# An attention and expert-layer block: operands turned by transposing transfers, and scatters that wait for their landings alone

## The chip, the cores and the metric

The kernel runs on one core of a Trainium2 chip. The metric is the device time of one execution in microseconds (us).

## What is computed

The input x has 8 batches of 512 tokens, each of 128 numbers. The block is attention without weight matrices, a layer norm, a routed expert layer with a shared expert beside it, and a second layer norm.

```python
xh = x.reshape(8, 512, 16, 8)                      # 16 heads of 8
c  = xh - mean(xh, axis=1)
p  = softmax(einsum('bthd,bThd->bhtT', c, c))
x  = layernorm(x + einsum('bhtT,bThd->bthd', p, xh))   # "x1" in the kernel

scores = sigmoid(x @ gate_weight.T)                # 64 experts
# top 4 of 8 groups by (scores + bias), then the top 8 experts of them
# a token gets a slot of an expert while fewer than 128 tokens have one, in the order of tokens
ye  = (silu(xe @ w1.T) * (xe @ w3.T)) @ w2.T       # for each expert, its 128 slots
out = sum over a token's 8 experts of weight * ye
out = out + (silu(x @ sg.T) * (x @ su.T)) @ sd.T   # shared expert
x   = layernorm(x + out)
```

## The kernel before

Every instruction is placed by hand on its engine, and engines wait for each other's counters (semaphores). A counter of a transfer rises by 16 when the transfer has landed. Each engine, SP's queue of transfers included, does its list strictly in order.

**Stage 1, attention and routing, batch after batch.** TensorE, ScalarE and VectorE run through batches b = 0 to 7. In a batch, TensorE makes 32 blocks of scores (`score`, L664), two matmuls of 512 columns each, into four banks S, so that two blocks are in flight. ScalarE takes each with one exponential (L913) into `large`, and TensorE weighs the values with it (`weigh`, L678) into PV. A batch has 16 slots of two scores; at fixed slots (`SLOT_OF`) TensorE does small jobs into two other banks, M[0] and M[1] (`BANK`): for the next batch q = b + 1 the mean (`mean`), the largest norm (`most`) and the turned operands (`lr0` to `lr7`), and for the previous batch p = b - 1 what leads to its routing (`xt`, `logits`, `gate`, `up`, `down`, `pos`, `totals`). A job waits until the reader of the job before it in its bank is through.

The operands of the scores are split in three bf16 parts. VectorE writes them for batch q into AK and AQ (`prep_parts`, `prep_rows`; the last step is `l40`), tokens on partitions. The scores need them with tokens along the row: job `lr`j turns two heads of both by 8 transposing matmuls (L582) into a bank, and VectorE (six of them, `take_turned`, L1173) or ScalarE (j = 3 and 6, L891) copies the bank into LR. The copies of j = 0 to 7 happen while LR's earlier columns are still read by the scores of batch b.

For batch p, VectorE computes x1 (L1187), the scores of the experts, the top 8, and at its end the slot numbers `index` (L1314). Then GpSimd writes the batch's records with 32 indirect transfers of 128 rows each (`scatter`, L506): a record is x1, the 64 weights and the token's number. GpSimd copies x1 into the record (L495) and makes the number (L496, L498). Each transfer waits for two things:

```python
wait(pool, exp_done, min(CHUNKS * (p + 2) + i * TOP + k - 4, CHUNKS * BATCHES))
landed = scattered[p % 2][k % 2]
wait(pool, landed, scatters_before(p) + 16 * ((i * TOP + k) // 2))
```

that is, until ScalarE has done a certain exponential of batch p + 2, and until the transfer two before it has landed. There are two record buffers; VectorE writes x1 of batch p once GpSimd has copied x1 of batch p - 1. A record whose slot number is out of bounds is dropped by the transfer; the experts' 128 slots fill up in the early batches.

**SP** loads x, clears `records` and `sums` in device memory, loads w1, w3 and w2 (L407 to L409), and then stores Z of each batch p (x1 plus the shared expert, L414) when VectorE has written it.

**Stage 2.** TensorE turns the experts' weights (L783), with ScalarE and VectorE copying them, while GpSimd still scatters. **Stage 3** begins when all scatters have landed: SP loads the slots of four experts at a time (L424), 16 steps; GpSimd adds the results to `sums` (L526). **Stage 4** is the last sum and layer norm.

## Time and profile before

| | |
|---|---|
| median of 3 runs | 682.28 us (682.13 to 687.41) |
| the profiled execution | 683.21 us, of which 681.5 us are the span of the trace |
| TensorE busy | 418.1 us, 61% of the span |
| GpSimd busy | 384.5 us, 56% |
| ScalarE busy | 382.2 us, 56% |
| VectorE busy | 343.8 us, 50% |
| chain that ended last | TensorE 23%, GpSimd 22%, ScalarE 20%, issue 17%, VectorE 15% |

The busy shares are means over stages that have different limits, so the view by stages says more than the table. In the trace PE is TensorE, PEld its weight loads, ACT ScalarE, DVE VectorE, POOL GpSimd, and SPq the queue of SP. "Issue" in the chain is time in which an engine waited for nothing that the profile shows.

### The profile page before, as it was taken

What the parts mean: (1) busy time and instruction counts of PE and PEld (TensorE: products, weight loads), DVE (VectorE), ACT (ScalarE), POOL (GpSimd) and SP (SyncE); (2) the same over time, 40 slices, a digit from 0 to 9 for tenths busy, and PEclk for the clock granted to TensorE, in tenths of its full rate; (3) what the DMA queues carried; (4) which work ended last, traced back from release to release, by engine and by line L of the source; (5) the groups of instructions that cost most, each with busy time, mean ns of one, the idle gap of its engine ahead of it and who ended that gap; (6) DMA issues with size and microseconds to landing.
All of it is one profiled execution on the core that took longest, in us unless ns stands there. A gap on an engine that the chain in (4) does not pass through costs nothing.

```text
span 681.5 us, 9076 instructions
## 1 busy us (share of the span) xinstructions
PE 418.1 (61%) x2948; PEld 194.5 (29%) x2948; DVE 343.8 (50%) x1118; ACT 382.2 (56%) x516; POOL 384.5 (56%) x424
## 2 busy tenths in 40 slices
PE   4788978968978878788798833352005546653000
PEld 4223323323322323232232212242005545542000
DVE  5514765766757757757742831863003343333065
ACT  2898958968969969879779931023003322210026
POOL 2000005566666667557566567566660888888846
PEclk9999979989979989989989975577557767675555
DMA  3899971110000000000000000000006555444498
GB/s 93 203 241 295 178 149 49 36 27 8 10 22 7 6 20 4 5 19 3 4 20 3 19 2 2 18 1 1 1 1 183 104 83 87 52 36 37 41 265 227
DMA packets 83125, 43.66 MB, mean 64 GB/s; under 512 B 13319, under 2 KB 82707, under 8 KB 83072
## 3 DMA queue, kind: packets, MB, share of 16 engines
q1 hardware_dynamic: 61568, 36.18, 22.2%
q0 software_dynamic: 21504, 6.81, 8.8%
q8 instruction: 29, 0.48, 0.3%
q14 instruction: 24, 0.20, 0.1%
HBM read 21.27 MB, written 44.40 MB: 96 GB/s over the span
## 4 chain that ended last, share of the span: by engine, by line
PE 23%; POOL 22%; ACT 20%; issue 17%; DVE 15%; DMA 3%; SPq 0%; ACTq 0%; POOLq 0%; DVEq 0%
ACT large L913 14%; POOL sums L526 14%; POOL records L506 8%; PE PV L678 8%; PE S L664 5%; PE M L582 2%; ACT OT L898 2%; PE M L570 1%; PE PV L688 1%; PE M L611 1%; DVE LR L1173 1%; PE M L605 1%; PE S L582 1%; DVE last_stats L1502 1%; DVE left L1267 1%
## 5 line engine op out<-in xcount | busy, mean ns | idle before, releaser
L506 POOL DMA_INDIRECT records<-rec,index x256 | 254.4, 994 | 175.7 <-ACT large L913 78.9
L913 ACT ACTIVATE large<-S,shift_now 128x1024 f32<-128x1024 f32 x256 | 274.7, 1125 | 59.6 <-PE S L664 59.1
L678 PE MATMUL PV<-large,V 128*9 128x512 f32 x1024 | 139.5, 618 | 0.2 <-ACT large L913 0.2
L526 POOL DMA_INDIRECT sums<-centred,target x64 | 99.9, 1561 | 35.8 <-issue 18.9
L664 PE MATMUL S<-LR 64*128 64x512 bf16 x512 | 101.5, 398 | 21.9 <-ACT large L913 19.0
L664 PEld LDWEIGHTS S<-LR 64*128 64x128 bf16 x512 | 24.4, 93 | 164.8 <-ACT large L913 123.0
L982 ACT COPY AK<-S 128x512 f32<-128x512 f32 x16 | 9.3, 583 | 67.2 <-PE S L792 67.2
L1173 DVE COPY LR<-M 128x1024 bf16<-128x1024 bf16 x42 | 28.7, 684 | 34.9 <-PE M L582 34.9
L792 PE MATMUL S<-ident,X 128*128 128x128 f32 x64 | 14.4, 369 | 48.5 <-DMA X<-records 48.5
L495 POOL COPY rec<-x 128x512 f32<-128x512 f32 x7 | 4.9, 699 | 67.0 <-DVE x L1187 67.0
L810 PE MATMUL PV<-ident,AK 128*128 128x128 f32 x32 | 9.0, 375 | 44.3 <-DVE AK L1444 44.3
L1469 DVE CAST target<-number 128x4 uint32<-128x4 f32 x16 | 2.7, 171 | 63.7 <-DMA sums<-centred,target 62.8
L688 PE MATMUL PV<-ident,OT 128*128 128x128 f32 x128 | 21.0, 286 | 14.1 <-ACT OT L898 14.1
L1021 ACT ACTIVATE last_log<-last_moments,eps 128x4 f32<-128x4 f32 x8 | 2.4, 297 | 46.5 <-DVE last_moments L1505 46.5
L997 ACT ACTIVATE X<-X 128x256 f32<-128x256 f32 x16 | 6.7, 417 | 36.7 <-DVE X L1433 36.7
L1458 DVE COPY weight<-X 128x4 f32<-128x4 f32 x16 | 2.6, 160 | 48.0 <-DMA X<-records 48.0
L816 PE MATMUL M<-large,AK 128*128 128x256 f32 (+1 forms) x64 | 26.4, 560 | 0.0
L792 PEld LDWEIGHTS S<-ident,X 128*128 128x128 f32 x64 | 11.4, 195 | 51.9 <-issue 50.3
L678 PEld LDWEIGHTS PV<-large,V 128*9 128x9 f32 x1024 | 15.2, 88 | 32.4 <-issue 28.5
L1071 DVE RECIPROCAL rden<-PV 128x16 f32<-128x16 f32 x32 | 8.1, 253 | 32.4 <-PE PV L688 32.4
L801 PE MATMUL S<-large,AK 128*128 128x128 f32 (+1 forms) x128 | 23.4, 343 | 0.0
L582 PE MATMUL M<-ident_b,AK 128*128 128x128 bf16 x224 | 22.9, 227 | 0.0
(184 smaller groups left out, 737.6 us busy)
## 6 DMA issues: line engine op xcount, KB each, us to landing
records<-blank SPq DMA_DIRECT2D x1, 6176.0 KB, 30.1
X<-records SPq DMA_DIRECT2D x16, 386.0 KB, 3.5
large<-sums SPq DMA_DIRECT2D x24, 256.0 KB, 4.7
sums<-blank SPq DMA_DIRECT2D x2, 2112.0 KB
large<-L_ffn_w_dram SPq DMA_DIRECT2D x2, 2048.0 KB, 21.3
records<-rec,index POOLq DMA_INDIRECT x256
X<-L_attn_x_dram SPq DMA_DIRECT2D x8, 256.0 KB, 2.8
sums<-Z SPq DMA_DIRECT2D x8, 256.0 KB
```

What stands on the lines that cost most here:

```text
L506: pool.indirect_dma_start(records, bass.IndirectOffsetOnAxis(ap=index[:, i * TOP + k:i * TOP + k + 1], axis=0), rec[:, i, :], None, bounds ...
L526: pool.indirect_dma_start(sums[n % SUMS], bass.IndirectOffsetOnAxis(ap=target[:, u, i:i + 1], axis=0), ye[:, u, i, :], None, bounds_check= ...
L582: mm = pe.transpose(bank[:, side * TOKENS + i * P:side * TOKENS + (i + 1) * P], A[:, i, 2 * j:2 * j + 2, :].rearrange("p a c -> p (a c)"), ...
L664: mm = pe.matmul(S[:, 2 * (n % 2) + j, :], LR[rows, pair, 0, tile * P:(tile + 1) * P], LR[rows, pair, 1, :], start=True, stop=True)
L678: mm = pe.matmul(PV[g % 2][32 * i:32 * i + VCOLS, :], V[:, 2 * c + k, QUAD * g + i, :], E[:, u % 2, i, k, :], start=c == 0 and k == 0, sto ...
L688: mm = pe.transpose(PV[g % 2][:, i * P:(i + 1) * P], OT[:, i * P:(i + 1) * P], ident[:, :])
L792: mm = pe.transpose(S[:, u % 2, i * CAP:(i + 1) * CAP], slots_in[:, u % 4, i * REC:i * REC + DIM], ident[:, :])
L801: mm = pe.matmul(S[:, 2 + u % 2, i * P:(i + 1) * P], xeT[:, u % 2, i * CAP:(i + 1) * CAP], w13_flat[:, bass.ds((GROUP_OF * s + i) * P, P)] ...
L816: mm = pe.matmul(M[u % 2][:, 2 * r * DIM:(2 * r + 2) * DIM], ehT[:, u % 2, r * CAP:(r + 1) * CAP], w2bd_flat[:, bass.ds((2 * s + r) * 2 * ...
L898: nc.scalar.copy(OT[:, :], PV[g % 2][:, :]).then_inc(quad_copied, 1)
L913: nc.scalar.activation(E[:, u % 2, 2 * (i // 2):2 * (i // 2) + 2, i % 2, :], S[:, 2 * (n % 2):2 * (n % 2) + 2, :], ACT.Exp, bias=shift_now ...
L1173: v.tensor_copy(LR[:, j, :, :].rearrange("p a t -> p (a t)"), Mb[bank]).then_inc(read[bank], 1)
```

## The change

Turning the operands moves from TensorE to SP. For each batch q from 1 on, SP issues two transposing transfers (`dma_start_transpose`, one for AK and one for AQ, each 128 partitions by 4096 bf16), once VectorE's `l40` of q is done and once the last score of batch q - 2 is done, since there are now two buffers LRs. Batch 0 is turned by TensorE as before. Jobs `lr0` to `lr7` go, with their copies on VectorE and ScalarE. TensorE waits at the start of a batch for both transfers (`turned`), and so does VectorE before it overwrites AK and AQ. `most` moves from slot 10 and bank 0 to slot 12 and bank 1. Z has two buffers and its store a counter for each. VectorE writes x1 and the number straight into the record, once the scatters of batch p - 2 have landed. GpSimd's copies go, and a scatter waits for `index` and for the landing of the one two before it; the wait for an exponential is gone.

```diff
-BANK = {"mean": 1, "lr0": 0, "lr1": 1, "xt": 0, "gate": 1, "logits": 0, "up": 0, "lr2": 1, "down": 0, "most": 0, "lr3": 1,
-        "pos": 0, "lr4": 1, "totals": 0, "lr5": 1, "lr6": 0, "lr7": 1}
-SLOT_OF = {"mean": 0, "lr0": 3, "lr1": 4, "xt": 5, "logits": 6, "gate": 6, "up": 7, "lr2": 9, "down": 9, "most": 10, "lr3": 11,
-           "pos": 12, "lr4": 13, "totals": 13, "lr5": 14, "lr6": 15, "lr7": 15}
+BANK = {"mean": 1, "xt": 0, "gate": 1, "logits": 0, "up": 0, "down": 0, "most": 1, "pos": 0, "totals": 0}
+SLOT_OF = {"mean": 0, "xt": 5, "logits": 6, "gate": 6, "up": 7, "down": 9, "most": 12, "pos": 12, "totals": 13}
-ACT_TAKES = {3: 11, 6: 15}
...
-PREP_JOBS = [name for name in SLOT_OF if name in ("mean", "most") or name.startswith("lr")]
+PREP_JOBS = ["mean", "most"]
...
-        AK = sb("AK", [P, TILES, HEADS, HEAD_ROWS], BF16)
-        AQ = sb("AQ", [P, TILES, HEADS, HEAD_ROWS], BF16)
-        LR = sb("LR", [P, HEADS // 2, 2, TOKENS], BF16)
+        A = sb("A", [P, 2, TILES, HEADS, HEAD_ROWS], BF16)
+        AK, AQ = A[:, 0, :, :, :], A[:, 1, :, :, :]
+        LRs = [sb(f"LR{k}", [P, 2, TILES, HEADS // 2, P], BF16) for k in range(2)]
...
@@ -408,11 +400,23 @@
+            def turn(q):
+
+                sp.wait_ge(prep, prep_at(q, "l40"))
+                if q >= 2:
+                    sp.wait_ge(scored, CHUNKS * (q - 1))
+                for side in range(2):
+                    sp.dma_start_transpose(LRs[q % 2][:, side, :, :, :].rearrange("p i j t -> p (i j) t"),
+                                           A[:, side, :, :, :].rearrange("p i h c -> p (i h c)")).then_inc(turned, 16)
+
+            turn(1)
             for q in range(BATCHES):
+                if q + 2 < BATCHES:
+                    turn(q + 2)
                 bank, n = job("epilogue" if q == BATCHES - 1 else "last" if q == BATCHES - 2 else "mid", q + 1, "down")
                 sp.wait_ge(read[bank], n + 1)
                 sp.dma_start(sums[0][q * TOKENS:(q + 1) * TOKENS, :].rearrange("(i p) d -> p i d", p=P),
-                             tokens_of(Z, q).rearrange("p (i d) -> p i d", i=TILES)).then_inc(dram_blank, 16)
+                             Z[:, q % 2, :, :]).then_inc(z_stored[q % 2], 16)
             for k in range(2):
...
@@ -488,19 +492,9 @@
             def scatter(p):
 
                 rec, index = record_of(p)
-                wait(pool, post, post_at(p, "x1_3"))
-                for t in range(2):
-                    wait(pool, scattered[p % 2][t], scatters_before(p))
-                if not last_of_all(p):
-                    nc.gpsimd.tensor_copy(rec[:, :, 0:DIM], x1[:, :, :]).then_inc(record, 1)
-                nc.gpsimd.tensor_copy(rec[:, :, TOK_COL], token[:, :]).then_inc(record, 1)
-                wait(pool, record, 3 * p + 3)
-                nc.gpsimd.tensor_scalar(token[:, :], token[:, :], float(TOKENS), None, ALU.add).then_inc(record, 1)
-                wait(pool, record, 3 * p + 4)
                 wait(pool, post, post_at(p, "index"))
                 for i in range(TILES):
                     for k in range(TOP):
-                        wait(pool, exp_done, min(CHUNKS * (p + 2) + i * TOP + k - 4, CHUNKS * BATCHES))
                         landed = scattered[p % 2][k % 2]
...
@@ -512,11 +506,11 @@
-            pool.wait_ge(small_ready, 3)
-            pool.sem_inc(record, 1)
             iterations(pool, batch)
             scatter(BATCHES - 1)
-            pool.wait_ge(dram_blank, 16 * (SUMS + BATCHES))
+            pool.wait_ge(dram_blank, 16 * SUMS)
+            for k in range(2):
+                pool.wait_ge(z_stored[k], 16 * BATCHES // 2)
 
...
@@ -583,17 +577,11 @@
-            def turn(phase, b, q, j):
-                if j == 0:
-                    wait_next(pe, prep, prep_at(q, "l40"))
-                m = begin(phase, b, f"lr{j}")
-                turn_into(Mb[m], j).then_inc(written[m], 1)
-
...
                     rows = slice(HEAD_ROWS * j, HEAD_ROWS * (j + 1))
-                    mm = pe.matmul(S[:, 2 * (n % 2) + j, :], LR[rows, pair, 0, tile * P:(tile + 1) * P],
-                                   LR[rows, pair, 1, :], start=True, stop=True)
+                    mm = pe.matmul(S[:, 2 * (n % 2) + j, :], LRs[b % 2][rows, 0, tile, pair, :],
+                                   LRs[b % 2][rows, 1, :, pair, :], start=True, stop=True)
                 mm.then_inc(scored, 1)
...
                 wait(pe, prep, prep_at(b, "shift"))
+                wait(pe, turned, 16 * 2 * b)
                 row_maxima(phase, b)
...
                                [:, :, lo:hi, :]).then_inc(v_built, 1)
-                bank, n = job(phase, b, f"lr{j}")
-                wait(act, written[bank], n + 1)
-                nc.scalar.copy(LR[:, j, :, :].rearrange("p a t -> p (a t)"), Mb[bank]).then_inc(read[bank], 1)
 
             def copy_quad(b, g):
...
             iterations(act, batch)
             copy_quad(BATCHES - 1, QUADS - 1)
             norm_start(BATCHES - 1)
             copy_x1T("epilogue", BATCHES)
-            act.wait_ge(post, post_at(BATCHES - 1, "x1_3"))
-            for t in range(2):
-                act.wait_ge(scattered[(BATCHES - 1) % 2][t], scatters_before(BATCHES - 1))
-            nc.scalar.copy(record_of(BATCHES - 1)[0][:, :, 0:DIM], x1[:, :, :]).then_inc(record, 1)
             exp_gate("epilogue", BATCHES, BATCHES - 1)
             exp_logits("epilogue", BATCHES, BATCHES - 1)
...
                 wait(dve, read[bank], n + 1)
+                wait(dve, turned, 16 * 2 * (q - 1))
                 x3 = xc[:, :].rearrange("p (g d) -> p g d", d=HD)
...
@@ -1182,9 +1151,12 @@
-                wait(dve, record, 3 * p + 1)
-                for i in range(TILES):
-                    t.step(f"x1_{i}", v.tensor_scalar(x1[:, i, :], O[:, i, :], moments[:, i, 0:1], rstd[:, i:i + 1],
+                rec, _ = record_of(p)
+                for way in range(2):
+                    wait_next(dve, scattered[p % 2][way], scatters_before(p))
+                t.step("number", v.tensor_scalar(rec[:, :, TOK_COL], rec[:, :, TOK_COL], 2.0 * TOKENS, None, ALU.add))
+                for i in range(TILES):
+                    t.step(f"x1_{i}", v.tensor_scalar(rec[:, i, 0:DIM], O[:, i, :], moments[:, i, 0:1], rstd[:, i:i + 1],
...
@@ -1273,8 +1245,10 @@
             def post_shared_out(phase, b, p):
                 bank, n = job(phase, b, "down")
                 wait_next(dve, written[bank], n + 1)
-                v.tensor_tensor(tokens_of(Z, p), M[bank][:, :], x1[:, :, :].rearrange("p i d -> p (i d)"), ALU.add
-                                ).then_inc(read[bank], 1)
+                wait(dve, z_stored[p % 2], 16 * (p // 2))
+                v.tensor_tensor(Z[:, p % 2, :, :],
+                                M[bank][:, :].rearrange("p (i d) -> p i d", i=TILES), record_of(p)[0][:, :, 0:DIM],
+                                ALU.add).then_inc(read[bank], 1)
...
                 rec, _ = record_of(p)
-                for way in range(2):
-                    wait_next(dve, scattered[p % 2][way], scatters_before(p))
...
-                    take_turned(phase, b, 2)
                 if with_post:
                     post_top(p, t)
                     post_shared_out(phase, b, p)
                     post_record(p, t)
+                leave(b, 1)
                 if with_prep:
                     take_most(phase, b, q)
-                leave(b, 1)
                 if with_post:
                     post_pos(phase, b, p, t)
-                if with_prep:
-                    take_turned(phase, b, 4)
                 if with_post:
                     post_totals(phase, b, p)
                 if with_prep:
-                    take_turned(phase, b, 5)
                     prep_shift(phase, b, q, w.step, w.after)
```

**SP's queue.** Around the end of the weight loads it held the following before (`w2n` is the last load of weights, Z the stored sum):

```order
12 L408 DMA large<-L_ffn_w_dram 64x64x128
13 L409 DMA w2n<-L_ffn_w_dram 128x64x64
14 L414 DMA sums<-Z 128x4x128 [waits read0] x8
15 L424 DMA X<-records 128x4x193 [waits scattered1_0,scattered1_1,scattered0_1,scattered0_0]
```

and now:

```order
12 L400 DMA large<-L_ffn_w_dram 64x64x128
13 L401 DMA w2n<-L_ffn_w_dram 128x64x64
14 L409 DMA_TRANSPOSE LR<-A 128x32x128 [waits prep]
15 L409 DMA_TRANSPOSE LR<-A 128x32x128
16 L409 DMA_TRANSPOSE LR<-A 128x32x128 [waits scored,prep]
17 L409 DMA_TRANSPOSE LR<-A 128x32x128
18 L418 DMA sums<-Z 128x4x128 [waits read0]
19 L409 DMA_TRANSPOSE LR<-A 128x32x128 [waits scored,prep]
```

The first pair, for batch 1, stands behind the clearing of the buffers and all loads of weights; the later pairs stand each ahead of a store of Z.

**TensorE's queue** in the later half of a middle batch (slots 9 to 11) before:

```order
134 L582 MATMUL M<-ident_b,AQ 128x128 x4
135 L624 MATMUL M<-small_T,hT 128x128 x4
136 L664 MATMUL S<-LR 128x512 x2
137 L678 MATMUL PV<-large,V 9x512 x4
138 L664 MATMUL S<-LR 128x512 x2
139 L688 MATMUL PV<-ident,OT 128x128 x4
140 L576 MATMUL M<-largest_diag,ones 128x128
141 L664 MATMUL S<-LR 128x512 x2
```

and now (slots 9 to 12):

```order
92 L612 MATMUL M<-small_T,hT 128x128 x4
93 L650 MATMUL S<-LR 128x512 x2
94 L664 MATMUL PV<-large,V 9x512 x4
95 L650 MATMUL S<-LR 128x512 x2
96 L674 MATMUL PV<-ident,OT 128x128 x4
97 L650 MATMUL S<-LR 128x512 x2
98 L664 MATMUL PV<-large,V 9x512 x4
99 L650 MATMUL S<-LR 128x512 x4
100 L664 MATMUL PV<-large,V 9x512 x4
101 L650 MATMUL S<-LR 128x512 x2
102 L570 MATMUL M<-largest_diag,ones 128x128
103 L622 MATMUL M<-mask_b,before_b 128x64 x2
```

The turning matmuls are gone, and the matmul of `most` no longer follows `down` at once in the same bank; it stands four scores later, ahead of `pos`.

**GpSimd's queue** at the first batch's scatters before (`rec` is the record, `index` the slot numbers):

```order
28 L495 COPY rec<-x 128x4x128 [waits records_blank,small_ready,post]
29 L496 COPY rec<-token 128x4
30 L498 TENSOR_SCALAR token<-token 128x4 [waits record]
31 L506 DMA records<-rec,index 8192x193 [waits exp_done,post,record]
32 L506 DMA records<-rec,index 8192x193 [waits exp_done]
33 L506 DMA records<-rec,index 8192x193 [waits scattered0_0,exp_done]
```

and now:

```order
28 L500 DMA records<-rec,index 8192x193 [waits post,records_blank]
29 L500 DMA records<-rec,index 8192x193
30 L500 DMA records<-rec,index 8192x193 [waits scattered0_0]
31 L500 DMA records<-rec,index 8192x193 [waits scattered0_1]
32 L500 DMA records<-rec,index 8192x193 [waits scattered0_0]
```

What is left on the queue is the transfers, each with one wait.

## Rows read from the trace of the kernel before

**Rows 1.** The page's busy tenths in 40 slices of the span.

```profile
PE   4788978968978878788798833352005546653000
POOL 2000005566666667557566567566660888888846
```

**Rows 2.** Busy time of each engine by stretch: batch 5, batch 7, two later stretches.

```profile
257.50:307.10 49.60, 41.58 (x321) 15.30 (x321) 33.03 (x105) 40.31 (x49) 31.60 (x33) 0.93 0.05 10
357.30:397.60 40.30, 34.48 (x252) 9.95 (x244) 21.68 (x81) 38.93 (x47) 24.91 (x28) 1.00 0.05 10
475.00:513.10 38.10, 0.00 (x0) 0.00 (x0) 0.00 (x0) 0.00 (x0) 25.25 (x26) 0.50 0.02 1
513.10:681.50 168.40, 64.92 (x288) 54.22 (x288) 64.85 (x256) 44.93 (x112) 116.87 (x120) 0.63 0.59 113
```

**Rows 3.** Timeline of VectorE and GpSimd around the scatters and the slot numbers.

```profile
102.22 0.18 DVE L1314 TENSOR_SCALAR index<-best 128x32 uint32<-128x32 f32 x1
...
103.72 1.23 POOL L506 DMA_INDIRECT records<-rec,index  x1 [29.46 <-ACT large L913]
...
393.64 0.22 DVE L1314 TENSOR_SCALAR index<-best 128x32 uint32<-128x32 f32 x1
...
416.52 1.12 DVE L1187 TENSOR_SCALAR x<-O,moments,rstd 128x128 f32<-128x128 f32 x4 [12.46 <-POOL token L498]
...
440.20 0.18 DVE L1314 TENSOR_SCALAR index<-best 128x32 uint32<-128x32 f32 x1
...
466.57 1.06 POOL L506 DMA_INDIRECT records<-rec,index  x1 [0.57 <-POOL token L498]
```

**Rows 4.** The chain that ended last, in order of time: start, us, what.

```profile
435.73 2.69 DMA records<-rec,index
...
467.63 0.30 issue
467.94 0.90 POOL records L506
468.84 0.73 issue
...
511.01 2.10 DMA records<-rec,index
```

**Rows 5.** Groups of instructions in batch 5 (257.5 to 307.1 us).

```profile
L913 ACT ACTIVATE large<-S,shift_now 128x1024 f32<-128x1024 f32 x32 | 34.4, 1124 | 9.1 <-PE S L664 9.0
...
L582 PE MATMUL M<-ident_b,AK 128*128 128x128 bf16 x32 | 3.4, 231 | 0.0
...
L576 PE MATMUL M<-largest_diag,ones 128*128 128x128 f32 x2 | 0.8, 488 | 4.2 <-DVE Z L1276 4.2
```

**Rows 6.** The exponentials' group in batch 7 (357.3 to 397.6 us).

```profile
L913 ACT ACTIVATE large<-S,shift_now 128x1024 f32<-128x1024 f32 x32 | 34.4, 1120 | 1.1 <-PE S L664 1.0
```

**Rows 7.** Timeline of ScalarE at the starts of batches 1, 5 and 7.

```profile
59.06 0.20 ACT L904 COPY shift_now<-shift 128x1 f32<-128x1 f32 x1
...
257.44 0.20 ACT L904 COPY shift_now<-shift 128x1 f32<-128x1 f32 x1
...
357.32 0.20 ACT L904 COPY shift_now<-shift 128x1 f32<-128x1 f32 x1
```

**Rows 8.** Timeline of SP's queue: the issue of the last weights.

```profile
70.74 11.22 SPq L409 DMA_DIRECT2D w2n<-L_ffn_w_dram  x1
```

**Rows 9.** Transfers from 90 to 106 us, in 40 slices of 0.4 us: busy tenths, GB/s.

```profile
DMA  9999999999999964795100000000000000000034
GB/s 202 230 220 223 218 246 207 218 228 225 223 220 212 189 123 87 228 285 169 26 20 12 0 0 0 0 0 0 0 0 0 0 0 0 0 0 0 0 116 131
```

**Rows 10.** Transfers of SP's queue, 66 to 82 us: packets, MB, share of 16 engines.

```profile
q1 hardware_dynamic: 5529, 2.82, 119.0%
```

**Rows 11.** Transfers of GpSimd's queue, 400 to 512 us.

```profile
q0 software_dynamic: 3600, 0.14, 2.1%
```

**Rows 12.** Timeline of VectorE: the last step of `prep_rows` in batch 5.

```profile
263.88 0.28 DVE L1158 COPY AK<-AQ 128x512 bf16<-128x512 bf16 x1
```

More of the change, by code:

```diff
@@ L244, in post_norm_block @@
         dram_blank = sem("dram_blank")
+        z_stored = [sem(f"z_stored{k}") for k in range(2)]
         written = [sem(f"written{o}") for o in range(2)]
@@ L254, in post_norm_block @@
         first_turned = sem("first_turned")
+        turned = sem("turned")
         first_taken = [sem(f"first_taken{o}") for o in range(2)]
@@ L929, in batch @@
                         build_v(b, HEADS - QUAD, HEADS)
-                    if phase != "last":
-                        for j, at in ACT_TAKES.items():
-                            if slot == at:
-                                take_turned(phase, b, j)
                     if phase != "first":
@@ L1392, in _ @@
             v.tensor_copy(slot_base[:, :], slot_base_i[:, :]).then_inc(small_ready, 1)
[L1393 removed]
+            for k in range(2):
+                v.tensor_scalar(recs[k][:, :, TOK_COL], token_i[:, :], float((k - 2) * TOKENS), None, ALU.add
+                                ).then_inc(small_ready, 1)
             v.tensor_copy(blank[:, TOK_COL:REC], blank_i[:, :]).then_inc(small_ready, 1)
```

47 lines of the change are left out of this document (15 added, 32 removed).

## The prediction

> **What bounds the kernel now.** I read the 40 slices first, then the stretches, then the chain. In the slices [rows 1] (17 us each, counted from 0) TensorE is busy through slice 22, thin after it, idle in 28 and 29, and busy again from 30, while GpSimd never stops from slice 6 to 29. So there are three bounds in turn. Up to 397.6 us the batches bound; from there to 513.1 us the scatters do (in the last 38.1 us of it no other engine did anything [rows 2]); after that comes an expert stage that the change does not touch, 168.4 us [rows 2].
>
> The scatters. The chain shows what one costs: a landing 2.10 us after the start, then 0.73 us until the waiting transfer starts [rows 4]. Each waits for the one two before it, so a pair takes 2.83 us and more; the last group's 31 steps from 466.57 to 511.01 us [rows 3, 4] are 1.43 us each, 2.87 us a pair, whatever GpSimd's own 0.97 us. The last batch's 32 scatters ran from 466.6 to 513.1 us: 46.5 us [rows 3, 4]. The first started at 103.7 us, 1.3 us after the first `index` was done at 102.4 us [rows 3]. From there to 513.1 us are 409.4 us; eight groups at 46.5 us are 372 us. The difference is the wait for exponentials, which ties a group to a batch of attention: batches 1 to 6 take (357.3 - 59.1) / 6 = 49.7 us each [rows 7].
>
> The batches. In batch 5 ScalarE waits 9.0 us for scores, in batch 7 1.0 us [rows 5, 6]. Batch 7 is the batch without `lr`, `mean` and `most` jobs, and it takes 40.3 us [rows 2]. So it is a row for what a batch costs when nothing is turned.
>
> **What the change removes.** Per middle batch: 64 turning matmuls (6.7 us of TensorE; the group shown is half of them, the other half took as long [rows 5]), eight copies, and the wait of 4.2 us of `most` for Z in bank 0 [rows 5], which goes with its move to bank 1. `mean` and `most` stay: 1.1 + 0.8 us of matmuls beside batch 7's 40.3 us. A batch then takes 42.2 us, 7.5 us less than 49.7 us. The copies on ScalarE and VectorE lie beside this and are in batch 7's figure. `index` of the previous batch is ready 393.9 - 357.3 = 36.5 us after batch 7's start [rows 3, 7], so 38.4 us after a middle batch's start. GpSimd's copies, about 1 us a group, go from the path; VectorE's one small step more is under 0.2 us and has the batch to hide in.
>
> **What it adds: a hole before batch 1.** TensorE now waits at the start of batch 1 for the first pair of transposing transfers. They stand on SP's queue behind the clearing and the weights, whose last issue ends at 70.7 + 11.2 = 82.0 us [rows 8]. The transfers already queued keep the DMA engines at nine tenths until 96.0 us [rows 9]. Batch 1 starts at 59.1 us now [rows 7]. So nothing of attention runs between the end of batch 0 and 96 us plus the pair's own time T. Everyone waits for that: TensorE, ScalarE behind its scores, VectorE at its overwriting of AQ, and with them `index` of batch 0, thus GpSimd. The Trainium skill, "DMA: Bandwidth & Descriptors", section "Queues, rings and completion order", says that each DMA engine consumes the descriptors of SP's ring in ring order; by that the pair cannot overtake the weights.
>
> **The price of a pair.** Both transfers move 2 x 128 x 4096 x 2 bytes = 2.10 MB. No row shows a transposing transfer. From below: the fastest slice moves 285 GB/s [rows 9], which gives 7.4 us. From above: if the pair went in pieces as small as the scatters' packets, 3600 of them carry 0.14 MB (39 bytes each) and take 2.1% of 16 engines in 112 us, 10.5 ns each [rows 11]; 53,800 of them make 35 us. Between them: the weight loads moved 2.82 MB in 16 us, 176 GB/s [rows 10], in packets of some 512 bytes; AK's rows of 128 values are 256 bytes, so this row is nearest. It gives 11.9 us; with one landing of 2.1 us I take T = 14 us.
>
> **What the pairs cost later.** Those of batches 2 to 7 are issued 6.7 us into the batch before (VectorE's last step of `prep_rows` ends at 264.2 us in a batch that began at 257.4 us [rows 7, 12]) and have the other 35.5 us to land: hidden up to T = 35.5 us. But from batch 3 on they run beside scatters. A scatter beside a store of Z landed after 2.69 us, not 2.10 us [rows 4], so a pair of scatters takes 3.46 us, not 2.87 us, and 14 us of transposing cost 14 x 0.59 / 3.46 = 2.4 us. Five of them: 12 us. From below this is nothing (the store may not have been what held that landing); at T = 35 us it is 30 us.
>
> **The sum.** Batch 1 starts at 96 + 14 = 110 us; `index` of batch 0 at 148.4 us; first scatter 1.3 us later, 149.7 us, where it was 103.7 us. The batches then gain: six at 42.2 us and one at 40.3 us end at 404 us, about where they ended before (397.6 us). But `index` of batch p comes every 42.2 us and its scatters take 46.5 us, so GpSimd never catches up and works through eight groups without a gap: 372 us, and 3 us for groups whose records still carry data (first batches) = 375 us. The queue of scatters also holds VectorE back: x1 of batch p needs the record buffer of p - 2, which from batch 5 on is free some us late, and this too is beside GpSimd's work. The last `index` is out well before group 7's turn at about 480 us. End of the scatters: 149.7 + 375 + 12 = 536.7 us, 23.6 us later than 513.1 us. The rest, 168.4 us, is as it was. The profiled execution took 683.2 us; with 23.6 us it is 706.8 us. It stands 0.9 us above the median, so the median becomes **706 us**. With T at its lower end, and nothing lost to the pairs, the sum is 7 + 12 = 19 us less, 687 us. At T = 35 us it is 21 + 18 = 39 us more, 745 us.
>
> **Rivals.** (a) *Transposing is so slow that it sets the period.* Beyond T = 35.5 us a batch is 6.7 us + T, since AK and AQ cannot be filled again before the pair has landed and the next batch cannot start. With T = 70 us, twice the upper row, batch 1 starts at 166 us, batch 7 six times 76.7 us later at 626 us and ends at 666.5 us; the last `index` follows after 440.4 - 397.6 - 12.5 = 30.3 us (the 12.5 us were a wait for GpSimd [rows 3]) at 697 us, and its scatters end at 745 us, 232 us later than now: 914 us. For: nothing in the trace bounds a transpose from above except by my choice of pieces. Against: the DMA engines are idle after 100 us and 2 MB are little. Chance 0.13. The Trainium skill, "VectorE: DVE Perf Modes", section "The three transpose paths", gives 1309 ns for one 128 x 128 bf16 tile by DMA; 64 tiles one after another would be 84 us, an estimate, and the total near 1010 us. The same skill, "DMA: Bandwidth & Descriptors", section "Latency and other measured facts", gives 261 GB/s for one kernel's transposes, 8 us for a pair, and the total near 690 us. The two differ tenfold, and no run here shows either yet.
>
> (b) *The scatters get faster.* Each now carries two waits; the 0.73 us after a landing may hold the handling of the second, for a transfer that need not wait for a landing starts 0.30 us after the one before [rows 4]. If so, a pair shrinks to 2 x (0.97 + 0.30) = 2.54 us; 128 pairs gain 128 x 0.31 = 40 us: 666 us. Against: the 0.73 us begin when the landing is there, and the exponential was there long before. It decides from a pair 0.18 us shorter on (128 x 0.18 = 23.6 us). Chance 0.09.
>
> (c) *The first pair does not stand behind the loads,* only behind their issue: batch 1 starts at 82 + 14 = 96 us, 14 us earlier, and with nothing lost to the pairs, another 12 us: 680 us. Against: the engines are full until 96 us, so it could only take its share of them. Chance 0.10.
>
> (d) *Below 689 us by the forecast's own mechanism,* T and its contention both near their lower ends: 0.06. *Between 689 and 745 us:* 0.57. What is left, 0.05, is that the batches, run cold after the hole (a TensorE clock of 0.5 of full speed stands in idle stretches [rows 2]), or held by the scatters, end later than GpSimd needs them: 745 to 790 us.
>
> **How the numbers follow.** A measurement of this kernel can tell about 1% from no change, 6.8 us. Faster by more: (b) and a hundredth for the sharpest form of (c): 0.10. Within: the rest of (c), (d) low, and some of the forecast's lowest: 0.17. Slower: 0.73. The range leaves out (b) below and (a) above: 680 to 790 us.
>
> **What would show it.** In the profile after: TensorE and ScalarE idle from about 58 us to batch 1's start at 103 to 130 us, its first scores released by a transfer into LR; the transfer pair's time from issue to landing; exponentials' wait for scores down from 9 us to about 2 us a batch, a batch at 42 us if VectorE is not held by records, 46 us in the last ones; GpSimd's scatters without gaps at 1.43 us from about 150 us, longer where a pair runs; the end of scatters near 537 us; and the stretch after it still 168 us. The prediction is wrong if a middle batch is as long as a pair takes, if batch 1 starts near 60 us, or if a scatter takes under 1.4 us.

## The result and the profile after

The changed kernel takes **696.43 us** (median of 4 runs, 696.12 to 697.31), the kernel before 682.95 us beside it (median of 4). The ratio is 1.019, with a 95% interval of [1.014, 1.023]: slower, clear of no change, by about 2%. The profiled execution took 696.14 us, its span 694.1 us.

First the slices of the page, for TensorE and GpSimd (17.4 us each, counted from 0):

```profile
PE   4681028889859878758759795235304565563000
POOL 2000000044757657567567666777772688888846
```

TensorE is now idle in slice 4, where before it went straight on, and GpSimd starts in slice 8, not in 6 [rows 1]. In slices 25 to 29 its digit is 7, where it was 5 or 6 in the last slices of scatters before (0.97 us of work stands in 1.28 us, below). ScalarE's timeline shows the hole:

```profile
57.35 0.19 ACT L885 COPY shift_now<-shift 128x1 f32<-128x1 f32 x1
100.75 1.11 ACT L894 ACTIVATE large<-S,shift_now 128x1024 f32<-128x1024 f32 x1 [43.20 <-PE S L650]
```

Batch 1 is prepared at 57.35 us and computes its first exponential at 100.75 us, after 43.20 us without scores. What TensorE waited for stands in the chain (start, us, what), followed from SP's queue to the transfer into LR:

```profile
68.35 9.52 SPq L401
77.86 0.04 issue
77.91 13.85 SPq L409
91.76 0.05 issue
91.81 6.82 DMA LR<-A
98.63 1.39 issue
100.02 0.61 PE S L650 x2
```

L401 is the issue of the last weights, L409 that of the pair's first transfer. SP's queue was through with the weights' issue at 77.9 us and began the pair's at once, but the pair ended at 98.6 us. The transfers from 84 to 104 us, in 40 slices of 0.5 us (busy tenths, GB/s), show why:

```profile
DMA  9999999999999999999999999999000001000000
GB/s 340 336 346 334 340 346 332 344 325 248 228 268 231 224 217 217 221 176 218 218 216 217 220 217 215 222 218 206 18 0 0 0 0 33 0 0 0 0 0 0
```

Until about 88.5 us the engines moved weights and clearing at 340 GB/s. Then the rate changes to 220 GB/s and stays there until 98 us: that is the pair, behind everything queued before it. In the trace its 8192 packets of 256 bytes lie between 88.2 and 98.1 us. So the pair takes 9.9 us, 212 GB/s. The later ones meet no weights, only scatters and a store of Z. The window 149 to 163 us holds one of them:

```profile
DMA  5200779900029999999899989529999999999982
...
q1 hardware_dynamic: 8256, 2.10, 92.9%
q0 software_dynamic: 280, 0.56, 15.2%
...
LR<-A SPq DMA_TRANSPOSE x2
```

92.9% of 16 engines for 14 us are 208 us of packets, 25 ns for each of 8256 (by pairs the mean is 22 to 25 ns), more than twice the 10.5 ns of a scatter's packets [rows 11]. The six later pairs, like the first by their first and last packet of this size, take 10.0 to 11.7 us. The Trainium skill, "DMA: Bandwidth & Descriptors", section "Latency and other measured facts", has 261 GB/s for one kernel's transposes, thus 8 us, an estimate; this case shows 180 to 212 GB/s from a pair's first packet to its last. The 1309 ns for each 128 x 128 tile that the same skill gives in "VectorE: DVE Perf Modes", section "The three transpose paths", would have made 84 us, and no pair here is near it.

Next the scatters. The first pair beside them, on GpSimd's timeline (in brackets the idle time and what ended it):

```profile
148.80 1.13 POOL L500 DMA_INDIRECT records<-rec,index  x1 [0.43 <-DMA records<-rec,index]
150.24 0.97 POOL L500 DMA_INDIRECT records<-rec,index  x1 [0.31 <-issue]
153.70 0.97 POOL L500 DMA_INDIRECT records<-rec,index  x1 [2.49 <-DMA records<-rec,index]
157.44 0.97 POOL L500 DMA_INDIRECT records<-rec,index  x1 [2.78 <-DMA records<-rec,index]
159.04 0.97 POOL L500 DMA_INDIRECT records<-rec,index  x1 [0.63 <-DMA records<-rec,index]
163.41 0.97 POOL L500 DMA_INDIRECT records<-rec,index  x1 [3.39 <-DMA records<-rec,index]
```

Idle times of 2.5 to 3.4 us stand there, each ended by a landing. And this is the last group, beside nothing:

```profile
520.65 0.97 POOL L500 DMA_INDIRECT records<-rec,index  x1 [0.30 <-issue]
521.93 0.97 POOL L500 DMA_INDIRECT records<-rec,index  x1 [0.30 <-issue]
523.21 0.97 POOL L500 DMA_INDIRECT records<-rec,index  x1 [0.30 <-issue]
524.48 0.97 POOL L500 DMA_INDIRECT records<-rec,index  x1 [0.31 <-issue]
```

A scatter starts every 1.28 us, its own 0.97 us and 0.30 us of issue. Before it was 1.43 us [rows 3, 4], with 0.73 us of issue after the landing. The groups start at 141.1, 200.9, 244.9, 300.4, 351.9, 396.8, 442.0 and 484.1 us, and the last landing is at 526.6 us. Two batches and the expert stage by windows (PE, PEld, DVE, ACT and POOL busy, the granted clock, DMA share, GB/s):

```profile
143.90:185.20 41.30, 35.91 (x258) 11.36 (x258) 28.96 (x100) 39.00 (x47) 23.02 (x23) 1.00 0.46 91
331.60:386.00 54.40, 39.99 (x260) 12.01 (x258) 29.10 (x100) 39.60 (x46) 34.68 (x35) 0.87 0.26 47
526.60:694.10 167.50, 64.92 (x288) 54.35 (x288) 64.85 (x256) 44.82 (x112) 116.26 (x120) 0.64 0.58 113
```

Batch 2 takes 41.3 us where middle batches took 49.7 us [rows 2, 7]. Batch 6 takes 54.4 us with the same work in it. VectorE's timeline says what held it:

```profile
352.87 0.17 DVE L1157 TENSOR_SCALAR rec<-rec 128x4 f32<-128x4 f32 x1 [9.81 <-DMA records<-rec,index]
```

The record buffer that VectorE now fills itself was still being scattered, for 9.81 us. The expert stage takes 167.5 us, 168.4 us before [rows 2].

**The difference in one sum.** The scatters end at 526.6 us instead of 513.1 us, 13.5 us later, and the rest is 0.9 us shorter: 12.6 us of span, and the time went from 683.2 to 696.1 us. The start of the scatters is 37.4 us later (141.1 against 103.7 us), and from there to their end are 385.5 us instead of 409.4 us. The next runs ask for the parts of these two numbers.

### The profile page after: what moved, and what is told of

It reads as the page before. It is cut to its first block, busy times and chain, and to the rows that moved or that the text cites. A ratio compares the mean times of both kernels' runs of the same rounds, so it can differ in the third digit from the quotient of the medians.

```text
span 694.1 us, 7872 instructions
## 1 busy us (share of the span) xinstructions
PE 392.3 (57%) x2500; PEld 170.9 (25%) x2500; DVE 318.5 (46%) x1085; ACT 372.9 (54%) x501; POOL 375.1 (54%) x401
## 4 chain that ended last, share of the span: by engine, by line
POOL 37%; DMA 22%; issue 14%; SPq 11%; DVE 7%; PE 5%; ACT 4%; ACTq 0%; DVEq 0%; POOLq 0%
POOL records L500 23%; DMA records<-rec,index 17%; POOL sums L520 14%; SPq L395 4%; DMA X<-L_attn_x_dram 2%; ACT large L894 2%; SPq L409 2%; PE PV L664 1%; SPq L401 1%; SPq L398 1%; DMA LR<-A 1%; SPq L400 1%; PE S L650 1%; DVE last_stats L1467 1%; DMA large<-sums 1%
## 5 line engine op out<-in xcount | busy, mean ns | idle before, releaser
L650 PE MATMUL S<-LR 64*128 64x512 bf16 x512 | 99.8, 395 | 69.4 <-issue 46.6
L955 ACT COPY A<-S 128x512 f32<-128x512 f32 x16 | 9.3, 583 | 53.9 <-PE S L779 53.9
L1086 DVE TENSOR_TENSOR centred<-X,M 128x512 f32<-128x512 f32 x8 | 5.5, 688 | 67.6 <-PE M L564 67.6
L797 PE MATMUL PV<-ident,A 128*128 128x128 f32 x32 | 8.8, 369 | 44.1 <-DVE A L1409 44.1
L584 PE MATMUL M<-ident,rec 128*128 128x128 f32 x32 | 7.1, 360 | 43.2 <-DVE rec L1159 43.2
L803 PE MATMUL M<-large,A 128*128 128x256 f32 (+1 forms) x64 | 26.3, 559 | 0.0
L849 ACT COPY x1T<-M 128x512 f32<-128x512 f32 x8 | 4.7, 590 | 40.0 <-PE M L584 40.0
L788 PE MATMUL S<-large,A 128*128 128x128 f32 (+1 forms) x128 | 23.4, 344 | 0.0
L788 PEld LDWEIGHTS S<-large,A 128*128 128x128 f32 x128 | 22.8, 266 | 0.2
L1165 DVE TENSOR_SCALAR sg<-eg 128x512 f32<-128x512 f32 x8 | 3.5, 434 | 39.9 <-ACT eg L861 39.9
```

Source lines behind the costliest of these rows:

```text
L650: mm = pe.matmul(S[:, 2 * (n % 2) + j, :], LRs[b % 2][rows, 0, tile, pair, :], LRs[b % 2][rows, 1, :, pair, :], start=True, stop=True)
L788: mm = pe.matmul(S[:, 2 + u % 2, i * P:(i + 1) * P], xeT[:, u % 2, i * CAP:(i + 1) * CAP], w13_flat[:, bass.ds((GROUP_OF * s + i) * P, P)] ...
L803: mm = pe.matmul(M[u % 2][:, 2 * r * DIM:(2 * r + 2) * DIM], ehT[:, u % 2, r * CAP:(r + 1) * CAP], w2bd_flat[:, bass.ds((2 * s + r) * 2 * ...
L955: nc.scalar.copy(xeT[:, u % 2, :], S[:, u % 2, :]).then_inc(x_copied, 1)
```

## The experiments

All ratios are to the kernel before on the same chip.

**1. The first pair ahead of the loads.** TensorE's hole is said to be a matter of the queue's order alone.

```diff
+            turn(1)
             sp.wait_ge(setup, SETUP)
             sp.wait_ge(small_ready, 4)
...
             sp.dma_start(w2n[:, :, :], w2.rearrange("e h f -> h e f")).then_inc(weights_loaded, 16)
-            turn(1)
```

> The kernel after, with the first pair of transposing transfers (for batch 1) issued ahead of the clearing and the weight loads, not behind them. Theory: the start of the scatters is set by the hole before batch 1, and the scatters then take their 385 us whatever their start. Batch 1 starts near 58 us, not 100.5 us, the first scatter near 101 us, not 141.1 us, the scatters end near 487 us, and the time is about 656 us. Rival: the second pair now meets the queued weights, batch 2 starts some 8 us late, and the first scatters of data collide with them: about 665 us. Second rival: the end is set by the batches and not by the scatters, and the gain is under 20 us: above 676 us.

661.69 us (654.88 to 664.23), ratio 0.968 [0.964, 0.972]. ScalarE's timeline at batch 1's start, and GpSimd's first scatter:

```profile
56.96 0.19 ACT L885 COPY shift_now<-shift 128x1 f32<-128x1 f32 x1
59.04 1.11 ACT L894 ACTIVATE large<-S,shift_now 128x1024 f32<-128x1024 f32 x1 [1.89 <-PE S L650]
```

```profile
98.85 1.23 POOL L500 DMA_INDIRECT records<-rec,index  x1 [93.06 <-DVE index L1286]
```

The 43.20 us are 1.89 us, and the first scatter is 42.3 us earlier. 34.7 us of them reach the end by the medians, and 41.3 us in the profiled executions (696.14 and 654.88 us; the latter is the fastest of four that spread over 9 us). So the hole is the queue, and it costs more than the whole change loses. With the order mended, the rest of the change is a gain.

The new order has a smaller hole of its own, which the expectation's first rival named with 8 us. The pair of batch 2 is now the one behind the clearing and the weights. ScalarE's timeline at batch 2's start:

```profile
101.64 0.19 ACT L885 COPY shift_now<-shift 128x1 f32<-128x1 f32 x1
117.29 1.11 ACT L894 ACTIVATE large<-S,shift_now 128x1024 f32<-128x1024 f32 x1 [15.45 <-PE S L650]
```

The pair's packets lie between 102.4 and 113.9 us. GpSimd does not wait for it, since it is still busy with group 0 (98.85 to 157.9 us). An order with both pairs ahead of the weights was not run.

**2. A second wait that holds nothing.** Each scatter of the changed kernel gets back a second semaphore wait, for exponentials that were done long before.

```diff
+                        wait(pool, exp_done, CHUNKS * (p + 1))
                         landed = scattered[p % 2][k % 2]
                         wait(pool, landed, scatters_before(p) + 16 * ((i * TOP + k) // 2))
```

> The kernel after, with one more wait on each scatter, for the last exponential of batch p, which is long done when index of batch p is there. It can delay nothing by what it waits for. Theory (rival b of the prediction): the second wait itself costs what turned 1.28 us a scatter into 1.43 us; some 225 undisturbed scatters take 0.15 us more, about 34 us in all, and the time is about 730 us. Rival: a fulfilled wait is free, 696 us, and the pace of the kernel before came from where its waits pointed.

744.41 us (742.58 to 748.22), ratio 1.089 [1.084, 1.094]: 48.0 us more than without it, though no exponential was ever late. The theory holds, but its 730 us were too little. The chain in the last groups has the step of before again:

```profile
503.87 0.84 POOL records L501
504.70 0.73 issue
...
506.00 0.73 issue
506.73 0.84 POOL records L501
```

256 scatters at 1.43 instead of 1.28 us would be 38 us. The other 10 us lie in the groups before the last, which take 50 to 65 us each; why it is more there was not taken apart.

**3. The kernel before without the wait for exponentials,** its only change.

```diff
-                        wait(pool, exp_done, min(CHUNKS * (p + 2) + i * TOP + k - 4, CHUNKS * BATCHES))
```

> The kernel before, with the wait for an exponential taken off the scatters and nothing else. Theory: a group then takes 41 us from when its index is there, so groups of batches 0 to 6 fit into batches of 49.7 us and the last starts when index 7 is there, near 428 us; the scatters end near 470 us, not 513 us, and the time is about 640 us. Rival: the pace stays 1.43 us, a group 46.5 us, the end 476 us, and the time about 645 us. Second rival: the scatters close behind each other slow the attention (transfers or GpSimd's port against VectorE), and the gain is under 20 us.

656.92 us (655.07 to 657.99), ratio 0.959 [0.956, 0.963]. A gain of 26.6 us, 17 us short of what was expected. GpSimd's timeline shows 1.28 us a scatter in the last group. But its groups begin at 104.5, 154.3, 204.6, 254.5, 303.6 and 353.8 us, one for each batch of 50 us: they wait for their `index`, and groups 5 and 6 then take 46.7 and 45.2 us, not 41 us. In the kernel before, groups 0 to 4 took 52 to 54 us each, so that group 5 began at 367.6 us. So the faster scatters gain 13.7 us up to group 5, where they stop at the pace of the batches, and the other 11.8 us of the 25.5 us between the two ends of the scatters (513.1 and 487.6 us) in groups 5 to 7.

**4. The kernel before with that wait kept and made void.** This tells the two readings of experiment 3 apart, the tie to a batch and the handling of a wait.

```diff
-                        wait(pool, exp_done, min(CHUNKS * (p + 2) + i * TOP + k - 4, CHUNKS * BATCHES))
+                        wait(pool, exp_done, 1)
```

> The kernel before with the value of the second wait alone changed: each scatter waits for exponential 1, done long before, so that nothing ties a group to a batch, but the instruction still carries two waits. Theory A (handling a second wait is what costs, 1.43 to 1.6 us a scatter instead of 1.28): the groups stay at 46 to 50 us and 683 us shrinks little, 675 to 683 us. Theory B (the tie to the exponentials is what costs): it falls to the 657 us of the run without the wait.

682.96 us (681.14 to 684.97), ratio 0.999 [0.997, 1.001]. Nothing is tied any more and nothing is gained. The chain in its last group:

```profile
489.42 0.73 issue
490.15 0.83 POOL records L506
490.98 0.73 issue
491.71 0.57 POOL records L506
492.28 0.73 issue
```

and GpSimd's timeline there:

```profile
485.90 0.97 POOL L506 DMA_INDIRECT records<-rec,index  x1 [0.53 <-issue]
487.27 0.97 POOL L506 DMA_INDIRECT records<-rec,index  x1 [0.40 <-issue]
488.77 0.97 POOL L506 DMA_INDIRECT records<-rec,index  x1 [0.54 <-issue]
```

From 485.90 to 488.77 are 2.87 us for two, the landing 2.10 us after the start and 0.77 us more. With one wait two take 2.55 us, so that a scatter starts at most 0.45 us after the same landing. The ratios of the two runs differ by the whole gain of experiment 3. What it gained is the handling of a second wait, not the tie.

The traces also show what this handling is. L296 is the line of the helper `wait`, and the instructions of GpSimd that stand under it are, first in this run and then in experiment 3:

```profile
L296 POOLq EVENT_SEMAPHORE  x288: 17/17/27723, 75.1 to 673.4; - x144
L296 POOLq EVENT_SEMAPHORE  x36: 17/30/3458, 103.5 to 649.6; - x36
```

That is 252 more for 256 scatters. In the trace of this run a scatter itself carries the wait for the exponential, and the wait for the landing stands as an instruction of its own ahead of it, for instance at 488.02 us, 0.75 us before the scatter of 488.77 us. In the trace of experiment 3 the scatter carries the wait for the landing, and nothing stands between. So the second wait is an instruction more between the landing and the next scatter, and the 0.73 us of issue follow on it. The kernel before and experiment 2 have such an instruction for nearly each scatter too; the changed kernel has 29 in all. Whether less is lost when that instruction takes the fulfilled wait, and the scatter the landing, was not tried.

**5. The pairs beside scatters.** In the changed kernel those of batches 3 to 7 are left out and SP raises the counter in their place; these batches compute scores from stale operands.

```diff
+                if q >= 3:
+                    sp.sem_inc(turned, 32)
+                    return
                 for side in range(2):
```

> The kernel after, with the pairs for batches 3 to 7 left out: SP raises their counter itself, so all waits stay, and those batches use stale operands, so that their results are not the reference's (scatters and their number are the same). Theory: the five pairs delay scatters by 31 us in all (the sum of the gaps over 1.28 us inside their windows), so the time is about 665 us. Rival: the long gaps in the first groups are those of records that carry data, not of the pairs, and the gain is under 15 us: above 681 us.

669.68 us (663.63 to 673.25), ratio 0.976 [0.970, 0.981]. The five pairs cost 26.8 us by the medians, 5.4 us each, and not 12 us. In the trace after, the idle time of scatters over 1.28 us inside the five pairs' windows adds up to 31.1 us, 6.2 us a pair. Not all of it is the pairs': over all groups that time is 57.0 us in the trace after and still 33.2 us in this run's, 23.8 us less. That fits its profiled execution, 673.25 us, which is 22.9 us faster and the slowest of the four.

**6. Both costs out:** experiments 1 and 5 in one kernel (scores of batches 3 to 7 from stale operands again).

```diff
+            turn(1)
             sp.wait_ge(setup, SETUP)
...
+                if q >= 3:
+                    sp.sem_inc(turned, 32)
+                    return
```

> The changed kernel with both of its suspected costs taken out: the first pair stands ahead of the clearing and the weights, and the pairs of batches 3 to 7 are left out (those batches compute scores from operands of batches 1 and 2, so the output is not the reference's; only the time is asked for). Theory (hole and beside-scatters cost are separate and add): 696.4 - 34.8 - 26.8 = 634.8 us, and near the 629 us of the kernel with TensorE turning. Rival (they overlap, since with the hole gone the batches and not the scatters govern, and a lost 6 us beside a pair is then caught up): 645 us or more.

641.25 us (640.9 to 644.53), ratio 0.940 [0.936, 0.944]. The sum of the parts was 634.9 us: they add but for 6.3 us. It can be read in group 0. It takes 57.8 us (99.3 to 157.1), 48.7 us in experiment 10, where the weights have landed before it starts. Its 32 scatters take 5.3 us more (52.7 to 47.4 us from the first start to the last), beside the last weights and the pair of batch 2. And then GpSimd waits 4.08 us for `index` of batch 1, since batch 2 has the hole of experiment 1 again: 15.36 us without scores until 117.66 us. In experiment 1 GpSimd was not yet through with group 0 at that time.

**7. `most` in the other bank,** alone in the kernel before.

```diff
-BANK = {"mean": 1, "lr0": 0, "lr1": 1, "xt": 0, "gate": 1, "logits": 0, "up": 0, "lr2": 1, "down": 0, "most": 0, "lr3": 1,
+BANK = {"mean": 1, "lr0": 0, "lr1": 1, "xt": 0, "gate": 1, "logits": 0, "up": 0, "most": 1, "lr2": 1, "down": 0, "lr3": 1,
...
-SLOT_OF = {"mean": 0, "lr0": 3, "lr1": 4, "xt": 5, "logits": 6, "gate": 6, "up": 7, "lr2": 9, "down": 9, "most": 10, "lr3": 11,
+SLOT_OF = {"mean": 0, "lr0": 3, "lr1": 4, "xt": 5, "logits": 6, "gate": 6, "up": 7, "most": 8, "lr2": 9, "down": 9, "lr3": 11,
```

The changed kernel has `most` in bank 1 too, but at slot 12. Here the turning jobs still use the banks, and bank 1 is free at slot 8. VectorE takes it before `down` and not after.

> The kernel before with one part of the change alone: `most` moved from slot 10 and bank 0 to slot 8 and bank 1; TensorE still turns, and GpSimd still writes the records and waits for the exponentials. Theory (the 4.2 us of `most` lie on the batches' path, and the wait for exponentials ties a group of scatters to a batch): a middle batch shrinks from 49.7 to about 45.5 us; the groups then run at their own 46.5 us for 1.43 us a scatter, six of them 3.2 us shorter: about 683 - 19 = 664 us. Rival (ScalarE waits for the turning matmuls anyway, `most` hides behind them): batches stay at 49.7 us, 683 us.

679.44 us (677.47 to 681.01), ratio 0.994 [0.991, 0.996]: 3.9 us, not 19. Both expectations missed. The first batches did shrink, by more than said: batch 3 goes from 147.05 to 190.72 us, 43.7 us instead of 49.5 us. But from batch 4 on they are 52.5, 51.3 and 50.7 us. VectorE's timeline in batch 4 shows who holds them:

```profile
208.47 1.11 DVE L1187 TENSOR_SCALAR x<-O,moments,rstd 128x128 f32<-128x128 f32 x4 [5.56 <-POOL token L498]
```

GpSimd's `token` step stands behind the scatters of the group before, and its groups take 48 to 56 us beside attention, with two waits on each scatter, and not the 46.5 us of the undisturbed last group. So the shorter batches meet the scatters' pace and take it over, by way of the `token` step.

**8. `most` and the removed wait together** in the kernel before.

```diff
-                        wait(pool, exp_done, min(CHUNKS * (p + 2) + i * TOP + k - 4, CHUNKS * BATCHES))
...
+                if with_prep:
+                    take_most(phase, b, q)
```

> The kernel before without the wait for exponentials and with `most` at slot 8 and bank 1; TensorE turns, GpSimd copies. Theory: batches of 45.5 us bring `index` of the first groups 4.2 us earlier each, from where the scatters' own 44 to 46 us a group govern: last scatter at about 465 us instead of 485, 638 us. Rival (`most` is worth nothing): 657 us.

643.27 us (642.32 to 644.17), ratio 0.941 [0.937, 0.945]. Together they bring 40 us where one brings 26.6 and the other 3.9. Two middle batches by windows:

```profile
190.80:234.50 43.70, 39.60 (x321) 14.90 (x322) 32.38 (x105) 40.56 (x50) 29.75 (x31) 1.00 0.05 12
234.50:278.10 43.60, 39.50 (x321) 14.79 (x321) 32.15 (x105) 40.46 (x49) 29.90 (x32) 1.00 0.05 11
```

The same 321 matmuls as in the row of before (49.60 us, granted clock 0.93 [rows 2]) stand in 43.6 us, with a granted clock of 1.00. And ScalarE's exponentials in the second of them:

```profile
L912 ACT ACTIVATE large<-S,shift_now 128x1024 f32<-128x1024 f32 x32 | 34.5, 1125 | 2.9 <-PE S L663 2.8
```

The 9.0 us of waiting for scores [rows 5] are 2.8 us, with all turning still on TensorE. That is 6.2 us for moving one small job. A batch of the changed kernel waits 1.9 us there, so the turning itself was worth little: batches of 43.6 us become 41.3 us.

**9. VectorE writes the records,** in the kernel of experiment 3; GpSimd's copies go.

```diff
-                    nc.gpsimd.tensor_copy(rec[:, :, 0:DIM], x1[:, :, :]).then_inc(record, 1)
-                nc.gpsimd.tensor_copy(rec[:, :, TOK_COL], token[:, :]).then_inc(record, 1)
...
-                    t.step(f"x1_{i}", v.tensor_scalar(x1[:, i, :], O[:, i, :], moments[:, i, 0:1], rstd[:, i:i + 1],
+                    t.step(f"x1_{i}", v.tensor_scalar(rec[:, i, 0:DIM], O[:, i, :], moments[:, i, 0:1], rstd[:, i:i + 1],
```

> The whole change but for the turning and for `most`: TensorE turns as before, scatters wait for landings alone, VectorE writes the records itself and GpSimd's copies are gone. Against the run in which only the wait for exponentials was taken out (657 us). Theory: groups 0 to 4 there were bound by their `index` at 49.7 us a batch, so only in the last three groups do GpSimd's copies (1.3 to 2 us each) lie on the path: 652 us, between 649 and 655. Rival (VectorE, now held at x1 by the record buffer as in the changed kernel, 7 to 10 us a batch, delays the batches): 657 us or more, up to 670.

654.41 us (652.68 to 655.18), ratio 0.957 [0.953, 0.961]. 2.5 us less than experiment 3, and the intervals overlap: a small gain at most, and no loss as large as the rival's. The batches take 50 us as in experiment 3, so VectorE held by the record buffers does not delay them here.

**10. The whole change without its transfers:** TensorE turns, with the single buffers LR and Z of before; the wait and the records are as changed, `most` as in experiment 7.

```diff
-                for side in range(2):
-                    sp.dma_start_transpose(LRs[q % 2][:, side, :, :, :].rearrange("p i j t -> p (i j) t"),
-                                           A[:, side, :, :, :].rearrange("p i h c -> p (i h c)")).then_inc(turned, 16)
...
+                m = begin(phase, b, f"lr{j}")
+                turn_into(Mb[m], j).then_inc(written[m], 1)
...
+                nc.scalar.copy(LR[:, j, :, :].rearrange("p a t -> p (a t)"), Mb[bank]).then_inc(read[bank], 1)
```

> The whole change except the transposing transfers: TensorE turns as before, `most` at slot 8 and bank 1, scatters wait for landings alone, VectorE writes the records. Theory (the change's other parts are all gains, the transfers all its loss): groups at 43 to 45 us from 103 us on, end at about 457 us, 627 us, between 620 and 635. The changed kernel's 696 us would then be 627 + 42 for the hole + 27 for the five pairs. Rival (the parts overlap, since the record buffers hold VectorE and with it the batches): 645 us or more.

**629.23 us** (626.95 to 634.96), ratio 0.920 [0.916, 0.924], the fastest version. Batches 2 to 6 take 43.7 us each, and the last scatter starts here:

```profile
462.38 0.97 POOL L493 DMA_INDIRECT records<-rec,index  x1 [0.30 <-issue]
```

So the parts of the change, added one after the other by medians: the wait 683.5 to 656.9 us (-26.6), the records 654.4 us (-2.5), `most` 629.2 us (-25.2), and the transposing transfers in the place of TensorE 696.4 us (+67.2). Of the 67.2 us, experiments 1, 5 and 6 account for 55.2 us (696.4 to 641.3), the hole and the five later pairs. Of the 12 us that are left by the medians, the profiled executions of experiments 6 and 10 (640.90 and 634.96 us) show 5.9 us, and there group 1 begins 7.5 us later: it is what group 0 loses in experiment 6. The rest lies in the spread of experiment 10, whose profiled execution is the slowest of its four.

## Why the prediction was right where it was, and wrong where it was not

The forecast was 706 us for a measured 696.4 us, and slower; the main reason, the hole, holds. That the number came so near is luck: it is the sum of terms that were wrong in opposite directions, and by one of the prediction's own signs, a scatter under 1.4 us, its account was wrong.

**What bounds the kernel.** Three bounds in turn hold, and the expert stage stayed at 167.5 us. That GpSimd works through eight groups from its first `index` on without catching up holds too: from 141.1 to 526.6 us it had no gap other than landings.

**The batches, 42.2 us.** Batches that nothing held took 41.3 us after (2), and 40.9 to 42.6 us in experiment 5: right within 1 us. Its split was wrong. I gave `most` 4.2 us and thought the turning to be most of what is left. Experiment 8 gives `most` 6.1 us (49.7 to 43.6), and the turning 2.3 us (43.6 to 41.3). As said, none of it mattered in the changed kernel, where the batches ended at about 426 us and not at 404 us, held by the record buffers, beside the scatters.

**The hole.** The pair stood behind clearing and weights, as said. Two sizes were off, both to the good: the queued transfers ended at 88 us, not 96 us, and the pair took 10.4 us with its landing (88.2 to 98.6 us) and not 14 us. Batch 1's first scores came at 100 us for 110 us, the first scatter at 141.1 us for 149.7 us: 8.6 us. The row of 176 GB/s was the right neighbour but a little slow, and rival (a) fell with the first trace. Why the queued transfers were through 8 us earlier was not looked into.

**The pace of the scatters: the step that failed.** "Eight groups at 46.5 us", thus 1.43 us a scatter, was read from the last group and kept for the changed kernel. The 0.73 us of issue belong to the removed wait, which made an instruction more between a landing and the next scatter (experiment 4). At 1.28 us the 255 steps are 326.4 us where the forecast had 375 us, landing included: 48.6 us less. It is rival (b), which I priced about right (40 us) and gave 0.09, arguing "the exponential was there long before". Experiments 2 and 4 show that this is no argument, because a fulfilled wait costs as much. (Its working has two slips: 2.87 less 2.54 us are 0.33 us and not 0.31 us, and 128 x 0.18 are 23.0 us.) Taken alone, it would have made the change a gain. A reading of before fell with it: the 409.4 us of the scatters against eight times 46.5 us were put down to the tie to exponentials, and experiment 4, without a tie, has the same groups of 48 to 55 us.

**The price of the pairs beside scatters: too low.** 2.4 us each was taken from a scatter beside a store of Z, 0.59 us per pair of scatters. The trace shows 6.2 us each, 31.1 us in all for 12 us; by leaving them out it is 26.8 us by the medians and 22.9 us in the profiled executions. Idle times of 2.5 to 3.4 us stand where the row had 0.59 us. The upper bound in the text, 30 us, was about the right value.

**What the sum lacked.** Outside the pairs the scatters lost another 25.9 us to landings later than 1.28 us would have them, almost all of it while attention runs (the last two groups have about 2 us of it). The forecast had 3 us for this and had otherwise taken the undisturbed last group for all groups. Experiment 7 failed by the same step.

The bill, by the trace after: -8.6 (first scatter), -48.6 (pace, with the forecast's 3 us in it), +19.1 (pairs, at their upper value), +25.9 (the rest of the landings, at its lower one), +2.1 (the last landing, which the 46.5 us included) are -10.1 us, and 0.9 us less in the expert stage. The forecast was 10 us high, by terms of up to 49 us.

Two things stay open. What delays the landings outside the pairs was not tried. And why a scatter beside a transposing transfer lands so much later than beside a store was only seen, not taken apart.

## What to carry to other kernels

Before an operation is moved to another queue, look at what the queue still holds at that time: here 2.10 MB that need 10 us came 40 us late, since weights which TensorE first reads at 467 us stood ahead of them. And look whom the new order puts last: with the first pair ahead, the second one came 15 us late. Where a row is read for a pace, ask which waits it carries: one that is long fulfilled is not free on an indirect transfer (count the semaphore instructions beside it in the trace), and where such a transfer sets the time, waiting for one semaphore instead of two can be worth more than any work that is taken away. And when two bounds are close, try their removals together: `most` brought 4 us alone and 25 us once the scatters were faster.

## What the runs showed of the hardware

- A second semaphore wait on an indirect transfer of GpSimd costs, though fulfilled: it stands in the trace as an EVENT_SEMAPHORE of its own, 0.73 us before the transfer, and two scatters take 2.87 us instead of 2.55 us. Over 256 of them it was 26 us in the kernel before (656.9 against 683.0 us, experiments 3 and 4), where it partly lay beside batches, and 48 us in the changed one (experiment 2).
- A transposing transfer of bf16 from SBUF to SBUF, 2 x 128 x 4096, goes in 8192 packets of 256 bytes at 22 to 25 ns. It takes 9.9 to 11.7 us from its first packet to its last. SP's queue is held for about as long: the issue of one of the two transfers takes 4.9 to 6.3 us, and that of the first of all, behind the weights, took 13.85 us.
- One such pair delays scatters beside it by about 5 us in all (26.8 us for five by the medians, 22.9 us in the profiled executions).
- Without the 4.2 us stall of TensorE for VectorE in each batch [rows 5], the mean granted clock of a batch is 1.00, where it was 0.93 [rows 2], so that 2.4 GHz was granted throughout. 6.1 us were gained where the stall had shown 4.2 us.
